# Adding the scaled expert outputs in pairs on GpSimd before TensorE sums them

## The reference

```
x1 = _layer_norm(x + attn_out, ln1_w, ln1_b)
gates = softmax(x1 @ gate_w.T + gate_b)
_, top_idx = top_k(gates, 2)
top_gates = take_along_axis(gates, top_idx)
expert_outputs = einsum("bsd,efd->bsef", x1, expert_w) + expert_b
sel = take_along_axis(expert_outputs, top_idx[..., None], axis=2)
moe_out = sum(sel * top_gates[..., None], axis=2)
return _layer_norm(x1 + moe_out, ln2_w, ln2_b)
```

## Time and profile before

| what | value |
|---|---|
| median of 3 runs | 1815.76 us (1814.04 to 1816.18) |
| the profiled execution's own time | 1819.28 us |
| its span in the trace | 1817.5 us |
| PE busy | 1681.8 us (93%) |
| DVE busy | 1268.1 us (70%) |
| ACT busy | 1193.8 us (66%) |
| POOL busy | 182.9 us (10%) |
| the expert part of the stage | about 1337 to 1409 us from the span's start |

### The profile page before, as it was taken

The page is one execution under the profiler, slowest core; times in us unless marked ns, Lnnn a source line. Parts: engine busy times, 40 slices in busy tenths (PEclk is TensorE's granted clock), DMA queues, the critical chain, the costliest instruction groups (busy, mean ns, idle before and its releaser), DMA issues. The chain is left out here.

```text
span 1817.5 us, 25943 instructions
## 1 busy us (share of the span) xinstructions
PE 1681.8 (93%) x10028; PEld 794.6 (44%) x10028; DVE 1268.1 (70%) x1804; ACT 1193.8 (66%) x2436; POOL 182.9 (10%) x171
## 2 busy tenths in 40 slices
PE   6999999999999999869999999999885798699997
PEld 3433333333333333245444444455553465344443
DVE  4888888888888888167788678574464366255555
ACT  4588888888888888845677777777546554333432
POOL 1000000000000000040000000111344000000100
PEclk9899999999999999989899999999988799699999
DMA  1000000000000000010000000000100000212220
GB/s 62 1 1 1 1 1 1 1 1 1 1 1 1 1 1 1 1 47 1 1 1 1 1 1 1 1 1 2 37 1 1 12 1 18 103 48 93 99 91 20
DMA packets 7274, 29.98 MB, mean 16 GB/s; under 512 B 680, under 2 KB 2736, under 8 KB 4848
## 3 DMA queue, kind: packets, MB, share of 16 engines
q1 hardware_dynamic: 7152, 28.33, 4.2%
HBM read 27.15 MB, written 1.18 MB: 16 GB/s over the span
## 5 line engine op out<-in xcount | busy, mean ns | idle before, releaser
L883 DVE TENSOR_REDUCE a_part_max<-a_ps 128x2 f32<-128x1024 f32 x512 | 602.5, 1221 | 86.9 <-PE a_ps L685 86.3
L868 ACT ACTIVATE a_probs<-a_ps 128x512 f32<-128x512 f32 x1024 | 533.1, 614 | 131.1 <-PE a_ps L781 128.6
L883 DVE TENSOR_REDUCE f_part_max<-f_ps 128x2 f32<-128x1024 f32 (+3 forms) x320 | 327.8, 1062 | 121.1 <-PE f_ps L685 65.2
L781 PE MATMUL a_ps<-a_q_shift,a_KA 64*128 64x512 f32 x1024 | 367.6, 448 | 3.6 <-POOL a_q_shift L664 2.4
L868 ACT ACTIVATE f_probs<-f_ps 128x512 f32<-128x512 f32 (+3 forms) x640 | 300.3, 539 | 99.8 <-PE f_ps L781 48.1
L781 PEld LDWEIGHTS a_ps<-a_q_shift,a_KA 64*128 64x128 f32 x1024 | 166.3, 187 | 290.8 <-ACT a_probs L868 275.1
L685 PE MATMUL a_ps<-a_KA,a_q_open 64*128 64x512 f32 x1024 | 278.0, 468 | 4.4 <-DVE a_part_max L883 3.8
L799 PE MATMUL a_psO<-a_probs,a_VA 128*32 128x512 f32 x2048 | 275.5, 610 | 3.9 <-ACT a_probs L868 3.9
L781 PE MATMUL f_ps<-f_q_shift,f_KA 64*128 64x512 f32 (+3 forms) x640 | 224.0, 435 | 4.7 <-POOL f_q_shift L664 2.2
L685 PE MATMUL f_ps<-f_KA,f_q_open 64*128 64x512 f32 (+3 forms) x640 | 170.4, 431 | 5.1 <-DVE f_part_max L883 4.3
L781 PEld LDWEIGHTS f_ps<-f_q_shift,f_KA 64*128 64x128 f32 x640 | 106.2, 188 | 150.1 <-ACT f_probs L868 138.4
(11 more groups left out here) (321 smaller groups left out, 1782.2 us busy)
## 6 DMA issues: line engine op xcount, KB each, us to landing
t_c_all<-c_rows SPq DMA_DIRECT2D x16, 1024.0 KB, 7.7
experts_w<-in_experts SPq DMA_DIRECT2D x1, 3264.0 KB, 10.5
W<-in_weights SPq DMA_DIRECT2D x1, 1574.0 KB, 6.2
out<-X SPq DMA_DIRECT2D x4, 256.0 KB, 6.8
K<-in_consts SPq DMA_DIRECT2D x1, 644.0 KB, 6.9
R<-in_rows SPq DMA_DIRECT2D x1, 530.0 KB, 5.9
W<-in_weights SPq DMA_DIRECT2D x1, 512.0 KB, 6.7
mx_conv_rows<-in_conv_rows SPq DMA_DIRECT2D x1, 512.0 KB, 3.5
```

The costliest lines, as they stand in the source:

```text
L781: mm = pe.matmul(bank(r)[:, lo:512], g.KA[rows, 2 * n + jp, P * s:P * s + P], q_shift[rows, u % 2, jp, lo:512], start=True, stop=not diag)
L868: nc.scalar.activation(probs[:, st % 2, j, lo:512], bank(r)[:, lo:512], ACT.Exp, scale=SCALE).then_inc(ring_read, 1)
L883: dve.tensor_reduce(part_max[:, 4 * q + 2 * jp:4 * q + 2 * jp + 2, c], ps1[:, k % 2, :, 0:b - a], AX_X, ALU.max).then_inc(max_read, 1)
```

## The change

ScalarE's four scaled outputs of a tile are added in pairs by GpSimd (0 + 2 and 1 + 3, one instruction of 256 elements on 128 partitions, written back in place), and TensorE sums two instead of four. TensorE waits for the new semaphore `paired`. So that a pair step stands in GpSimd's queue for each tile, GpSimd's loop over blocks becomes a loop over tiles, and its other steps move: `power(1, b-1)` behind pair(4b+1), the affine part of block b-1 (`affine_2`) behind pair(4b+2), and `power(2, b-2)` with the five operations for `u_scale` (`scale_of`) behind pair(4b) of block b. After the loop `power(1, 3)` now stands ahead of `scale_of(2)`.

```
-                    pe.wait_ge(e_scaled, ACT_E * (t + 1))
-                    for e in range(ACT_E):
+                    pe.wait_ge(paired, t + 1)
+                    for e in range(2):
                         mm = pe.matmul(ps[:, 7, P * i:P * i + P], g.k("ident"), scaled[:, t % 2, e, :],
-                                       start=False, stop=(i == 3 and e == ACT_E - 1))
+                                       start=False, stop=(i == 3 and e == 1))
                     mm.then_inc(s_added, 1)
...
-                for b in range(NB):
-                    power(1, b, var2, rstd2)
+                def pair(t):
+
+                    pool.wait_ge(e_scaled, ACT_E * (t + 1))
+                    pool.tensor_tensor(scaled[:, t % 2, 0:2, :], scaled[:, t % 2, 0:2, :], scaled[:, t % 2, 2:4, :],
+                                       ALU.add).then_inc(paired, 1)
+
+                def affine_2(b):
                     pool.wait_ge(applied2, 4 * b + 4)
...
+                def scale_of(b):
                     power(2, b, var3, rstd3)
...
+                for t in range(NT):
+                    b, i = t // 4, t % 4
+                    pair(t)
+                    if i == 0 and b >= 2:
+                        scale_of(b - 2)
+                    if i == 1 and b:
+                        power(1, b - 1, var2, rstd2)
+                    if i == 2 and b:
+                        affine_2(b - 1)
+                power(1, NB - 1, var2, rstd2)
+                scale_of(NB - 2)
+                affine_2(NB - 1)
+                scale_of(NB - 1)
```

More of the change, by code:

```diff
@@ L991, in attention_tail_stage @@
         e_ps, e_added, e_scaled = g.sem("e2_expert_ps"), g.sem("e2_expert_added"), g.sem("e2_expert_scaled")
-        s_added, moe = g.sem("e2_scaled_added"), g.sem("e2_moe")
+        s_added, moe, paired = g.sem("e2_scaled_added"), g.sem("e2_moe"), g.sem("e2_scaled_paired")
         var2, nb2, applied2, rstd2 = (g.sem("ln2_" + x) for x in ("var", "minus_mean", "applied", "rstd"))
```

## The result

The changed kernel took 1831.13 us (median of four runs, 1829.55 to 1832.79), the kernel before beside it 1815.15 us: a ratio of 1.0088, 95% interval 1.0073 to 1.0102. It is slower by 16.0 us, where +12.0 was forecast; the time lies in the range of 1823 to 1832. The profiled execution took 1831.82 us against 1819.28, which is +12.5. Two numbers are therefore to be explained: the 12.5 us that the traces show, and the larger difference of the medians.

What follows compares the result with a forecast made beforehand. TensorE sets the pace up to 1365 us, then one chain through ScalarE, GpSimd and VectorE. Terms 1.2 + 4.5 + 4.0 + 2.3 = +12.0 us on 1815.76 gave 1827.8 us, range 1823 to 1832, 80%.

Steps and rivals of the forecast that it cites:

- mixture(3): Last block's mixture on VectorE: pair(15) and its sum run beside stats3(2) and add nothing.
- Blocks 2 and 3: Expert part: apply2 and the affine part delayed behind pair steps, +4.5 us in block 2 and +4.0 in block 3.
- The leftover steps: After the loop: scale_of(2) behind power(1, 3) puts apply2(3) 4.73 us after the variance instead of 2.43, +2.3 us.
- Blocks 0 and 1: Start of the expert part: pair(6) delays block 0's affine part; after 1.16 us of VectorE slack, +1.2 us.
- The port: VectorE beside pair(0) and pair(1): SBUF port shared with GpSimd holds up small operations, 0.6 us taken, bounds 0 to 1.4.
- unknown costs of the clock: Few matmuls on the chain, a last sum and a transposition per block: lower granted clock costs at most some 1.5 us more.
- Behind the stage: The stage after the expert part: as long as before, moved as a whole.
- Faster: Rival: TensorE sets the pace to the end, each sum saves 0.445 us, 1808.6 us; 3%.
- no change: Rival: GpSimd's moved steps fit into slack, such as apply3's 3.8 us wait on ScalarE, 1815.8 us; 4%.
- Half of it: Rival: no delay ahead of apply2 in blocks 2 and 3, 4.4 us drop out, 1823.4 us; 8%.
- contention and clock: Rival: all 16 pair steps hold up VectorE's PSUM work by half a step each, 5.8 us more, 1833.6 us; 5%.

Runs made afterwards that it cites:

- pure delay: Kernel before with ten additions on constants in GpSimd's queue ahead of scale_of(3), delaying only the stage's end; 1831.19 us beside 1818.39, ratio 1.0075.
- the two with the filler: Seventeen unread matmuls at the stage's end, on the kernel before (ratio 1.0004) and with pairs for tiles 0 to 7 only, moved steps ahead (0.9991).
- the best version: Against the kernel before: pairs for tiles 0 to 7 only, GpSimd's moved steps ahead of them, seventeen unread matmuls at the stage's end; 1815.61 us, ratio 0.9991.

## Why the prediction was right, and where its sizes were off

The mechanism came as predicted, and four sizes were off. In the traces the kernel is 12.5 us slower, where 12.0 was forecast. That the two are so near is in part luck: the terms that were counted came out 0.9 us too high together, and the two that were put at zero added 1.5. The starts of the same steps in the two traces give each term. The difference between them grows from row to row by what the term added:

| step | before | after | later by | growth | forecast |
|---|---|---|---|---|---|
| apply3(0) on ScalarE | 1367.67 | 1368.33 | 0.66 | 0.7 | 1.2 |
| apply2(1) | 1371.76 | 1374.54 | 2.78 | 2.1 | 2.2 |
| affine part, block 1 | 1373.48 | 1378.43 | 4.95 | 2.2 | 2.3 |
| apply2(2) | 1385.34 | 1392.39 | 7.05 | 2.1 | 2.2 |
| affine part, block 2 | 1387.06 | 1395.82 | 8.76 | 1.7 | 1.8 |
| mixture(3) on VectorE | 1391.11 | 1400.41 | 9.30 | 0.5 | 0 |
| apply2(3) | 1395.75 | 1407.29 | 11.54 | 2.2 | 2.3 |
| last copy_ut | 1408.05 | 1419.59 | 11.54 | 0.0 | 0 |

*Blocks 2 and 3* came as worked out, 0.1 us less at each step, because two GpSimd instructions follow each other without the gap of 0.07 us that was put between them (pair(9) starts at 1372.61, the power at 1373.29, 0.68 later). The moves of the power and of the affine part were tested apart: 4.3 us for the first as forecast (2 x 2.2), 2.2 us for the second, where 4.2 were expected; the waits for late sums, read above as the effect of the clock, took back the rest. The table shows that the steps themselves are of the right size; what they are worth when taken away singly can be less.

*The leftover steps*: 4.67 us from the variance to apply2(3) (1402.62 to 1407.29), forecast 4.73. The run with the old order confirms the step: 2.8 us less.

*Blocks 0 and 1* were put too high, 1.2 against 0.7. The port was one cause. Two rows of the changed kernel's timeline:

```profile
1342.96 0.77 POOL L1177 TENSOR_TENSOR f_A<-f_A 128x256 f32<-128x256 f32 x1 [0.42 <-ACT f_A L1250]
1343.18 0.63 DVE L1365 TENSOR_TENSOR e_mark<-e_mark,K 128x64 f32<-128x64 f32 x1
```

Only this operation was held up, by 0.40 us (0.63 against 0.23), where 0.6 was taken; pair(0) met reductions and only the end of one operation. GpSimd's pair step was itself 0.04 us longer than the others. The Trainium skill, SBUF — State Buffer, section Who interferes with whom, says that a VectorE instruction with two SBUF inputs contends with a GpSimd instruction that reads SBUF, and that the order of issue decides which of them is blocked. The rows agree: the pair step had started first, and the VectorE operation ended at 1343.81, just behind the pair step's end at 1343.73. The rest of the 0.5 us is spacing: the affine part started 0.69 us after pair(6) instead of 0.80 (1360.57 after 1359.88), and experts(1), late by the port, started 0.3 us late instead of 0.6.

*mixture(3)* was a term at zero ("pair(15) and its sum run beside stats3(2) and add nothing"). It added 0.5 us. pair(15) was late as foreseen, but the sum behind it ran at the lower clock, 1.22 us instead of 0.61, and VectorE waited 0.47 for it. The prediction had priced that under the unknown costs of the clock, at most 1.5.

*Behind the stage*, a term at zero too, the trace shows 0.96 us. The next stage's first TensorE work started at 1410.26 before and got the full clock at 1420.1, 9.8 us later; in the changed kernel it started at 1421.81 and got it at 1433.7, 11.8 us later. The windows of that work, before and after (the second ends 0.4 us behind the return of the clock, so its mean is 0.52):

```profile
1410.20:1420.10 9.90, 9.84 (x36) 8.24 (x37) 1.17 (x5) 0.58 (x1) 2.45 (x2) 0.50 0.15 53
...
1421.80:1434.10 12.30, 12.29 (x39) 9.13 (x40) 3.52 (x8) 2.25 (x5) 2.42 (x2) 0.52 0.11 45
```

Two microseconds more at half the clock are an estimated 1 us of work, which is what the trace shows. But it is not shown that the delay causes this. In the traces of the other runs the part behind the stage does not follow the end of the stage:

| run | end | full clock after | part behind the stage |
|---|---|---|---|
| changed kernel | +11.62 | 11.8 us | +0.96 |
| pure delay | +11.68 | 11.8 us | +0.90 |
| old order of the leftover steps | +8.81 | 11.1 us | +0.01 |
| two sums, no pairs | -2.12 | 11.9 us | +1.01 |
| four sums with pairs | +13.78 | 9.7 us | -2.49 |

A stage that ends 2.12 us sooner has the same 1 us behind it, and one that ends 13.78 us later has 2.49 less. The 0.96 us are thus within what this part varies by from one trace to another (2.8 us shorter to 1.7 us longer over all runs), and its cause stays open.

*From 12.5 to 14.6 or 16.0.* The traces show 12.5 us: 11.54 at the end of the stage and 0.96 behind it. The rest is between the profiled execution of before and its other runs, many of which have a higher mean clock and are up to 5 us faster. A longer stretch at 1.2 GHz lowers the mean by itself, by an estimated 0.003 for the 11.6 us here, so the changed kernel's 0.956 to 0.959 answer to 0.959 to 0.962 of the kernel before, the lower end of its runs. Why the kernel before gets a higher clock in some runs, and the changed kernel in none of its nine, stays open. It is not a matter of the long delay alone: the version with all moved steps first, 0.5 us later at the end of the stage, does not get it in eleven runs either. The traces do not help: every trace here is of an execution at 0.962 or lower but for the two with the filler.

*The rivals.* "Faster" and "no change" are excluded by the measured time, and their reasons by the run with two sums alone (2.1 us, not 7.1) and by the two runs in which a moved step stands ahead again. "Half of it" is excluded by the two waits of 2.01 us. Of "contention and clock", the contention is excluded: one operation was lengthened, and the multiply-adds of the experts took 1.12 us for three beside pair(2) (from 1346.81) as without it. The clock's share is the 0.5 us ahead of mixture(3) and perhaps that behind the stage.

## What to carry to other kernels

When a step with a wait is put into a queue that was nearly empty, the price is not its length (0.73 us here, on an engine that was busy 10% of the time) but what stands behind its wait; a step on a dependency chain should stand ahead of it. The order of the moved steps cost 11.1 of 11.6 us, and the same additions in another order cost 0.5. Before taking work off an engine that looks full (13.45 of 14 us), ask by the waits whom it keeps waiting: half of TensorE's summing matmuls were worth 2.1 us, not 7.1. And a microsecond won or lost in one stage need not arrive at the end of the kernel: here the part behind the stage varied by more than the best version won.

## What was not expected of the hardware

The granted clock fell in the middle of the expert part (a mean of 0.97 in the changed kernel's stretch from 1366 to 1380, where it was 1.00 before) when TensorE was busy 8.81 of 14 us. The expert matmuls caught by it took 3.56 us there (from 1379.09, where nothing waited for them) and 3.23 us in the run with the affine part first, instead of 1.88. Conversely, TensorE busy for 16 of 19 us right ahead of a stage did not save that stage's first 10 us from the lower clock: it fell at the barrier, where TensorE was idle for 2.24 us, and stayed down while TensorE was busy again (11.30 of the 12 us from 1408 on).
